# Front of an attention-and-experts kernel: part buffers, the place of unit 0's loads, later constant rows, where the casts run, and when row-max tiles start

## The reference, cut to what matters

```python
q = (x @ Wq).reshape(B, T, N_HEAD, HEAD_DIM).transpose(0, 2, 1, 3)
k = (x @ Wk).reshape(B, T, N_HEAD_KV, HEAD_DIM).transpose(0, 2, 1, 3)
v = (x @ Wv).reshape(B, T, N_HEAD_KV, HEAD_DIM).transpose(0, 2, 1, 3)
...
att = jnp.einsum('bhqd,bhkd->bhqk', q, k) * scale
att = att + alibi[None] + causal[None, None]
att = jax.nn.softmax(att.astype(jnp.float32), axis=-1)
y = jnp.einsum('bhqk,bhkd->bhqd', att, v)
...
x = _layernorm(x + attention(x))
x = _layernorm(x + ffn(x))      # top-1 router, 8 experts, shared expert
```

## Time and profile before

| | us |
|---|---|
| median of 3 runs | 575.14 |
| lowest, highest | 573.35, 577.24 |
| the profiled execution | 570.18 |
| its span, first to last instruction | 568.5 |

### The profile page before, as it was taken

One profiled execution on the slowest core, in us unless ns is written; L12 is line 12 of the kernel. 1 busy time (PEld: TensorE's weight loads), 2 busy tenths in 40 slices (PEclk: granted clock), 3 DMA queues, 4 the chain that ended last, 5 costly groups with the idle time before them and its releaser, 6 DMA issues.

```text
span 568.5 us, 7844 instructions
## 1 busy us (share of the span) xinstructions
PE 520.3 (92%) x2538; PEld 258.0 (45%) x2538; DVE 301.4 (53%) x630; ACT 223.3 (39%) x455; POOL 172.5 (30%) x240
## 2 busy tenths in 40 slices
PE   5858899999999999998987989999989999999991
PEld 2323233333333333332235664655666666656561
DVE  1449988888888888884025635212222332333332
ACT  2311067676767676767940012011112222222310
POOL 4421121412121212121201004970003455454543
PEclk9879599999999999999988799999999999999997
DMA  8489330665354536400223800221111212122210
GB/s 242 136 197 267 121 72 21 134 192 137 123 123 136 138 123 126 133 20 21 67 82 102 277 1 1 71 105 48 55 55 57 74 57 82 58 75 65 64 49 28
DMA packets 39374, 55.91 MB, mean 98 GB/s; under 512 B 5801, under 2 KB 26925, under 8 KB 39230
## 3 DMA queue, kind: packets, MB, share of 16 engines
q1 hardware_dynamic: 29706, 31.94, 21.3%
q0 software_dynamic: 5952, 19.56, 11.0%
q10 hardware_dynamic: 3680, 3.94, 2.5%
HBM read 36.72 MB, written 18.51 MB: 97 GB/s over the span
## 4 chain that ended last, share of the span: by engine, by line
PE 80%; DVE 9%; DMA 4%; ACT 3%; issue 1%; SPq 1%; POOL 1%; POOLq 0%; ACTq 0%; DVEq 0%
PE ps L684 14%; PE ps L513 12%; PE ps L488 11%; PE ps L604 10%; PE ps L502 10%; PE ps L703 7%; DVE mx L834 6%; PE ps L615 5%; PE ps L576 3%; PE ps L490 2%; PE ps L695 2%; ACT probs L759 2%; PE ps L593 1%; DMA qk_or_dn<-qparts 1%; DMA qparts<-tmp 1%
## 5 line engine op out<-in xcount | busy, mean ns | idle before, releaser
L834 DVE TENSOR_REDUCE mx<-ps 128x1 f32<-128x512 f32 (+4 forms) x312 | 183.6, 643 | 30.8 <-PE ps L490 22.7
L759 ACT ACTIVATE probs<-ps 128x512 f32<-128x512 f32 x288 | 152.9, 604 | 79.9 <-PE ps L502 79.7
L488 PE MATMUL ps<-qk_or_dn 127*128 127x512 bf16 (+3 forms) x384 | 122.4, 343 | 10.8 <-DMA qk_or_dn<-qparts 6.0
L502 PE MATMUL ps<-qk_or_dn 127*128 127x512 bf16 x288 | 100.5, 380 | 2.7 <-ACT probs L759 2.3
L1083 POOL TENSOR_SCALAR_AFFINE_SELECT probs<-probs 128x512 f32<-128x512 f32 x64 | 40.7, 636 | 175.8 <-ACT probs L759 175.8
L684 PE MATMUL ps<-wgu,tmp 128*128 x184 | 82.9, 593 | 0.1
L488 PEld LDWEIGHTS ps<-qk_or_dn 127*128 127x128 bf16 x384 | 38.0, 100 | 88.3 <-DVE mx L834 70.1
L513 PE MATMUL ps<-probs,Vs 128*32 128x512 f32 x576 | 76.7, 605 | 0.7 <-ACT probs L759 0.7
L490 PE MATMUL ps<-cb 128*128 128x128 bf16 x256 | 53.3, 232 | 0.0
L1015 DVE TENSOR_TENSOR tmp<-tmp,ps 128x512 f32<-128x512 f32 x23 | 15.8, 687 | 64.8 <-PE ps L684 64.8
L1127 POOL DMA_INDIRECT rows<-acc,tok x23 | 22.5, 980 | 87.1 <-DMA out<-rows,tok 44.0
(11 more groups left out here) (111 smaller groups left out, 460.1 us busy)
## 6 DMA issues: line engine op xcount, KB each, us to landing
wgu<-in_gu POOLq DMA_DIRECT2D x8, 1024.0 KB, 6.2
qk_or_dn<-qparts SPq DMA_DIRECT2D x48, 128.0 KB
yT<-yU SPq DMA_DIRECT2D x16, 256.0 KB, 2.1
qk_or_dn<-in_dn SPq DMA_DIRECT2D x8, 512.0 KB, 8.1
qparts<-tmp SPq DMA_DIRECT2D x8, 384.0 KB, 5.1
tmp<-xs SPq DMA_DIRECT2D x23, 128.5 KB, 2.5
tmp<-yT SPq DMA_DIRECT2D x34, 64.0 KB
xs<-rows POOLq DMA_DIRECT2D x1, 2056.0 KB, 12.7
```

Source lines behind the costliest of these rows:

```text
L488: mm = pe.matmul(o, q, K6[k][0:KROWS, k0:k0 + w], start=True, stop=not masked)
L502: pe.matmul(o, K6[k][0:KROWS, kb * P:(kb + 1) * P], Q6[k][0:KROWS, :, qi * P:(qi + 1) * P], start=True, stop=True).then_inc(s_st, 1)
L759: act.activation(probs[:, 4 * (s % 3) + p, :], ps[:, 4 + (4 * s + p) % SB, :], ACT.Exp, scale=SCALE).then_inc(s_exp, 1)
L834: dve.tensor_reduce(o, ps[:, a_bank(u, t), 0:nh * w].rearrange("p (h w) -> p h w", h=nh), AX.X, ALU.max).then_inc(s_amax, 1)
```

## The change

`parts0` becomes four buffers (`NP`), and `rest0` two. Unit 0's head and its constant rows are issued first, with nothing to wait for; its K and Q loads directly behind the store of job 3, once the four stores have landed, then unit 1's constant rows and head; unit 1's K and Q stay behind the stores of jobs 8 and 9 (`UNIT1_AT`), with unit 2's constant rows behind those. `FIRST_A` is 6: the tiles come in six lots. `LATE_AT` keeps the six later loads at jobs 9, 10, 11. From job 6 on (`ACT_CASTS`) the cast is done by ScalarE at the end of its job step. `s_one` is one semaphore per set, waited for by each unit's first tile.

```diff
--- before.py
+++ after.py
@@ -91,7 +91,10 @@
     (2, 1), (3, 1)]
 NJ = len(JOBS)
 UNIT0_JOBS = 4
-FIRST_A = 8
+NP = 4
+assert UNIT0_JOBS == NP and NJ % NP == 0
+FIRST_A = 6
+UNIT1_AT, LATE_AT, ACT_CASTS = 8, 9, 6
 A_TILES = row_max_tiles()
 NA = len(A_TILES) + 1
 GROUPS = 9
@@ -168,10 +171,10 @@
         cb = sb("cb", [P, CB_N], BF16)
 
         tmp = sb("tmp", [P, 4096 + 2 * (C + 1)])
-        t16 = tmp[:, 0:3 * 3 * CH // 2].bitcast(BF16)
-        parts0 = [t16[:, r * 3 * CH:(r + 1) * 3 * CH].rearrange("p (a t) -> p a t", a=3) for r in range(3)]
-        vT = tmp[NG * D:P, 3840:3840 + CH]
-        rest0 = [tmp[:, 2304 + r * CH:2304 + (r + 1) * CH] for r in range(3)]
+        t16 = tmp[:, 0:NP * 3 * CH // 2].bitcast(BF16)
+        parts0 = [t16[:, r * 3 * CH:(r + 1) * 3 * CH].rearrange("p (a t) -> p a t", a=3) for r in range(NP)]
+        rest0 = [tmp[:, 3072 + r * CH:3072 + (r + 1) * CH] for r in range(2)]
+        vT = tmp[NG * D:P, 4096:4096 + CH]
         yTc = [tmp[:, i * 1024:(i + 1) * 1024].rearrange("p (k t) -> p k t", k=KC) for i in range(3)]
         rdc = [tmp[0:NH, 3072 + i * CH:3072 + (i + 1) * CH] for i in range(2)]
         den = tmp[:, 4096:4096 + 256]
@@ -234,8 +237,8 @@
         s_xT = [sem(f"s_xT{i}") for i in range(NCH)]
         s_prj, s_ph, s_pr, s_pm, s_pl, s_vT, s_vps, s_vev = (
             sem(n) for n in ("s_prj", "s_ph", "s_pr", "s_pm", "s_pl", "s_vT", "s_vps", "s_vev"))
-        s_pw = [sem(f"s_pw{i}") for i in range(3)]
-        s_one, s_seen = sem("s_one"), sem("s_seen")
+        s_pw = [sem(f"s_pw{i}") for i in range(NP)]
+        s_one, s_seen = [sem(f"s_one{i}") for i in range(STEP)], sem("s_seen")
         s_qk = [sem(f"s_qk{i}") for i in range(STEP)]
         s_vinit, s_vs = sem("s_vinit"), sem("s_vs")
         s_aps, s_amax, s_split, s_mparts, s_mrow = (
@@ -347,6 +350,13 @@
                     max_rows(u + 1, (k + 1) % STEP, isinstance(u, int) and u == NU - 2)
                 store_y(u, 1)
 
+            def load_rows(i):
+
+                sp.dma_start(Q6[i][M_ROWS:ROW0, :, :].rearrange("p h t -> p (h t)"), one_d).then_inc(s_one[i], 16)
+                sp.dma_start(K6[i][0:M_ROWS, :], one_d[0:M_ROWS, 0:T]).then_inc(s_one[i], 16)
+                sp.dma_start(Q6[i][TH0:KROWS, :, :].rearrange("p h t -> p (h t)"), thq_d).then_inc(s_one[i], 16)
+                sp.dma_start(K6[i][TH0:KROWS, :], thk_d).then_inc(s_one[i], 16)
+
             def load_x(c):
                 sp.dma_start(xTc[:, c], xT_d[:, c * CH:(c + 1) * CH].rearrange("(k p) t -> p k t", p=P)
                              ).then_inc(s_xT[c], 16)
@@ -360,11 +370,8 @@
             sp.dma_start(cb[:], cb_d).then_inc(s_w0, 16)
             load_x(2)
             load_x(3)
-            for i in range(STEP):
-                sp.dma_start(Q6[i][M_ROWS:ROW0, :, :].rearrange("p h t -> p (h t)"), one_d).then_inc(s_one, 16)
-                sp.dma_start(K6[i][0:M_ROWS, :], one_d[0:M_ROWS, 0:T]).then_inc(s_one, 16)
-                sp.dma_start(Q6[i][TH0:KROWS, :, :].rearrange("p h t -> p (h t)"), thq_d).then_inc(s_one, 16)
-                sp.dma_start(K6[i][TH0:KROWS, :], thk_d).then_inc(s_one, 16)
+            load_rows(0)
+            load_unit_head(0, 0)
             for n in range(NJ):
                 sp.wait_ge(s_pl, n + 1)
                 c, k = JOBS[n]
@@ -374,21 +381,21 @@
                 else:
                     r, m, dst = b * NG * D, NG * D, kparts_d
                 sp.dma_start(dst[:, r:r + m, col:col + CH].rearrange("a r t -> r a t"),
-                             parts0[n % 3][0:m, :, :]).then_inc(s_pw[n % 3], 16)
-                if n == UNIT0_JOBS:
-                    for i in range(3):
-                        sp.wait_ge(s_pw[i], 16 * ((UNIT0_JOBS + 2 - i) // 3))
-                    load_unit_head(0, 0)
+                             parts0[n % NP][0:m, :, :]).then_inc(s_pw[n % NP], 16)
+                if n == UNIT0_JOBS - 1:
+                    for i in range(NP):
+                        sp.wait_ge(s_pw[i], 16)
                     load_unit_k(0, 0)
-                if n == UNIT0_JOBS + 1:
                     load_unit_q(0, 0)
-                if n == FIRST_A:
+                    load_rows(1)
                     load_unit_head(1, 1)
+                if n == UNIT1_AT:
                     load_unit_k(1, 1)
-                if n == FIRST_A + 1:
+                if n == UNIT1_AT + 1:
                     load_unit_q(1, 1)
-            for i in range(3):
-                sp.wait_ge(s_pw[i], 16 * NJ // 3)
+                    load_rows(2)
+            for i in range(NP):
+                sp.wait_ge(s_pw[i], 16 * NJ // NP)
             max_rows(0, 0)
             with sp.Fori(0, LOOPS, 1) as it:
                 for k in range(STEP):
@@ -517,6 +524,8 @@
             def some(todo, n):
                 for v, t in todo[:n]:
                     if t == 0:
+                        if v < STEP:
+                            pe.wait_ge(s_one[v], 64)
                         pe.wait_ge(s_qk[v % STEP], S_QK * (v // STEP + 1))
                     max_tile(v, v % STEP, t)
                 del todo[:n]
@@ -544,7 +553,7 @@
                 if n and JOBS[n - 1][1] == 2:
                     values(JOBS[n - 1][0])
                 if n == FIRST_A + 1:
-                    pe.wait_ge(s_one, 64 * STEP)
+                    pe.wait_ge(s_one[0], 64)
                     pe.wait_ge(s_qk[0], S_QK)
                 if n > FIRST_A:
                     for t in first_tiles(n - 1):
@@ -734,14 +743,20 @@
 
             later_loads = [(x_all[:], x_d, s_x), (wo[:], wo_d, s_wo), (rt[:], rt_d, s_wo), (wsg[:], sg_d, s_wsh),
                            (wsu[:], su_d, s_wsh), (wsd[:], sd_d, s_wsh)]
+            def cast_rest(n):
+
+                m = P if JOBS[n][1] < 2 else NG * D
+                act.wait_ge(s_pr, n + 1)
+                act.activation(parts0[n % NP][0:m, 1, :], rest0[n % 2][0:m, :], ACT.Copy).then_inc(s_pm, 1)
+
             for n in range(NJ):
                 c, k = JOBS[n]
                 m = P if k < 2 else NG * D
                 act.wait_ge(s_prj, n + 1)
-                if n >= 3:
-                    act.wait_ge(s_pw[n % 3], 16 * (n // 3))
-                act.activation(parts0[n % 3][0:m, 0, :], ps[0:m, 4 + n % 4, :], ACT.Copy).then_inc(s_ph, 1)
-                i = 2 * (n - FIRST_A - 1)
+                if n >= NP:
+                    act.wait_ge(s_pw[n % NP], 16 * (n // NP))
+                act.activation(parts0[n % NP][0:m, 0, :], ps[0:m, 4 + n % 4, :], ACT.Copy).then_inc(s_ph, 1)
+                i = 2 * (n - LATE_AT)
                 for dst, src, done in later_loads[i:i + 2] if i >= 0 else []:
                     act.dma_start(dst, src.rearrange("(k p) n -> p k n", p=P)).then_inc(done, 16)
                 if k == 2:
@@ -750,6 +765,8 @@
                     act.activation(vT, ps[NG * D:P, 4 + n % 4, :], ACT.Copy).then_inc(s_vT, 1)
                 if n and JOBS[n - 1][1] == 2:
                     put_values(JOBS[n - 1][0])
+                if n >= ACT_CASTS:
+                    cast_rest(n)
 
             def weights(u, s):
                 for p in range(4):
@@ -836,13 +853,14 @@
 
             for n in range(NJ):
                 m = P if JOBS[n][1] < 2 else NG * D
-                h, md, rest = parts0[n % 3][0:m, 0, :], parts0[n % 3][0:m, 1, :], rest0[n % 3][0:m, :]
+                h, md, rest = parts0[n % NP][0:m, 0, :], parts0[n % NP][0:m, 1, :], rest0[n % 2][0:m, :]
                 dve.wait_ge(s_ph, n + 1)
-                if n >= 3:
-                    dve.wait_ge(s_pl, n - 2)
+                if n >= 2:
+                    dve.wait_ge(s_pl, n - 1)
                 dve.tensor_tensor(rest, ps[0:m, 4 + n % 4, :], h, ALU.subtract).then_inc(s_pr, 1)
-                dve.wait_ge(s_pr, n + 1)
-                dve.tensor_copy(md, rest).then_inc(s_pm, 1)
+                if n < ACT_CASTS:
+                    dve.wait_ge(s_pr, n + 1)
+                    dve.tensor_copy(md, rest).then_inc(s_pm, 1)
                 if n >= FIRST_A:
                     for t in first_tiles(n):
                         reduce_tile(0, t)
@@ -1051,7 +1069,7 @@
             for n in range(NJ):
                 m = P if JOBS[n][1] < 2 else NG * D
                 pool.wait_ge(s_pm, n + 1)
-                pool.tensor_tensor(parts0[n % 3][0:m, 2, :], rest0[n % 3][0:m, :], parts0[n % 3][0:m, 1, :],
+                pool.tensor_tensor(parts0[n % NP][0:m, 2, :], rest0[n % 2][0:m, :], parts0[n % NP][0:m, 1, :],
                                    ALU.subtract).then_inc(s_pl, 1)
             pool.wait_ge(s_vinit, 2)
             pool.wait_ge(s_vev, NCH)
```

## The result

| | before | after |
|---|---|---|
| median, beside each other on one chip | 574.80 us (573.35 to 577.24) | 584.93 us (583.91 to 585.27) |
| profiled execution; its span | 570.18; 568.5 | 585.27; 583.5 |
| first score matmul starts | 71.3 | 75.4 |
| first to last score matmul | 218.2 | 223.5 |
| last score matmul to the end | 279.0 | 284.6 |

The ratio is 1.0169 [1.0131, 1.0207]. The forecast was 571.7 and at most 575.8. All three parts of the span grew: the front by 4.1 us, the middle, which I had called unchanged, by 5.3, and the end by 5.6.

The account below looks back on a forecast made before the run. Front bound by a buffer wait and transfers until 37.7, then VectorE; VectorE would end at 29.8 + 1.1 + 25.2 + 3.75 = 59.85, but the last store sets scores at 67.9, 3.4 us earlier: median 571.7, range 566.0 to 575.8.

Parts of the forecast that it names:

- Four buffers: Front, job 3: its copy no longer waits for a store, so its store is issued at 19.2, not 21.99.
- Unit 0's loads behind its stores: Front, SP's queue: unit 0's Q lands at 29.8 against 37.7, 7.9 us gained.
- spent between 77 and 78, 7.3 us after the first issue: Unit 2's load, the same nine transfers alone, taken as measure for unit 0's landing: 21.9 + 7.3 = 29.2.
- rival 2: Front: gain eaten in transfers, unit 0's Q at 33.6 or later landings 3 us late; gain -0.5 to 1, 575; chance 0.09.
- The price inside VectorE's stretch: Front, VectorE: 25.2 us of work plus 3.75 us of idling, 1.85 of it at job 8.
- the other place: Front, chunk 3's transposes behind job 10 wait for ScalarE's vT of job 9: cost 1.9 us, 0 if wo's issue is short.
- What is late next: End of front: unit 1's Q costs 0.5 us, the last store delays the maxima; scores start at 67.9, not 71.3.
- 11 us after its first issue: Unit 1's Q: landing time read from the trace of before, near 57.5; now near 60, wanted at about 59.5.
- by 66.6 with the worst landing seen (8.9 us): Job 11's store, issued at 57.7, ahead of the maxima: latest landing 66.6, 64.8 taken.
- The middle unchanged: Long middle: TensorE busy 58.49 of 60 us at full clock, so it can't make up or lose time.
- Rival 3 (the clock): Front: TensorE's clock at half for most of the stage makes it the bound; 1.5 to 2.5 us slower, 577; chance 0.07.
- Rivals 1 and 4: Front: 1, gain nearly whole, 568, chance 0.25; 4, job 3's copy held by something else, 574.6, chance 0.02.

Follow-up runs that it names:

- e3: The changed kernel with SP waiting for unit 0's operands before issuing unit 1's constant rows and the stores of jobs 4 to 6: 581.05 us, 1.0157 to before.
- e4: The changed kernel with the six later loads issued by GpSimd in units 0 and 1, not by ScalarE: 575.26 us, 1.0023 to before.
- g2: The changed kernel with only the six later loads moved, issued by GpSimd from unit 6 on: 572.82 us, 0.9958 to before.
- h1: The changed kernel with 16 satisfied waits (eight instructions) ahead of ScalarE's loop and FIRST_A 7, later loads left in place: 573.64 us, 1.0004 to before.
- e1: The kernel before with ten satisfied waits (five instructions) added ahead of ScalarE's loop: 581.22 us, 1.0118 to before.
- e2: The changed kernel with 16 satisfied waits (eight instructions) added ahead of ScalarE's loop: 577.91 us, 1.0067 to before.

## Why the prediction was wrong

The sum for the medians: front +4.1 to +4.5 (71.3 and 70.9 in two profiles of before, 75.4 after; 3 to 3.5 of it by the change, counted from job 1's store), loop +5.3, which leaves 0.3 to 0.7 of the measured 10.1 for the end. Front and loop are single profiles here, so the split is good to about 1 us.

**Four buffers: right.** The copy of job 3 waits for no store, and the store goes out at 20.05 (19.2 forecast; 18.57 to 20.27 over the runs with the new order).

**Unit 0's loads behind its stores: mechanism right, the term mis-sized.** The step that failed is "spent between 77 and 78, 7.3 us after the first issue". I took the fall of the throughput for the landing. There the last load was issued at about 75.7 (three K loads stood behind Q), and the trace of before itself had the tail that e3 shows: SP's queue still moves packets until 80, as in (columns as in the earlier trace rows)

```profile
78.00:79.00 1.00, 1.00 (x11) 0.31 (x4) 0.70 (x2) 0.34 (x1) 0.06 (x1) 1.00 0.23 74
```

and only at 80 are all DMA engines idle, nearly 10 us after the first issue. In e3 a few engines carry the last packets for 2 us after the throughput has fallen. From the last Q issue to its landing it was 6.86 us, nearly the upper bound's 6.63, not 2.8: Q at 34.2, not 29.8, a gain of 3.4 and not 7.9. Job 5's store, ahead of Q before and behind it now, made no difference that shows: 6.63 to 6.85 us in the five profiles with the old order of loads, 6.66 to 8.29 in the nine with the new one. The sign that the prediction had named for rival 2, Q landing after 32, came true.

**The price inside VectorE's stretch: right in sum.** 28.1 us from first to last reduction against 28.95 worked out; job 8's idle 2.20 (1.85 forecast), the other place 0.53 (1.9 forecast; wo's issue held ScalarE 2.06 us, not 3, and e4, without that issue, has the same 0.53). VectorE ended at 63.5; with Q's error of 4.4 us put in, my own sum gives 64.3.

**What is late next: the right place, too small.** Forecast for the first score was 67.9. The 4.4 us by which unit 0's Q was late move nearly everything behind it (x at 45.95 for 42.3, unit 1's Q at 52.75 for 48.9), which gives 72.3 at most; the remaining 3.1 us are the landings. The step that failed is "11 us after its first issue": unit 1's Q took 14.6. And "by 66.6 with the worst landing seen (8.9 us)": the last store took 10.9 and the one before it 13.7. A landing time seen in another mixture of transfers is no upper bound. e4 and g2 show that the later loads are what it collides with (4.4 and 4.9 us), h1 that one lot of tiles fewer in front gives as much back at the first score and 3.5 us at the last. Rival 2 names this; it had 0.09, and it stopped at 3 us of lateness and at a time about that of before (575).

**"The middle unchanged": wrong, and no rival named it.** The argument was that TensorE is full there. What failed is that step: TensorE also depends on ScalarE, whose code had moved. 5.3 of the 10.1 us are this, and by e1 up to 6.6. With the gap taken out (e2) the change is still slower, by 0.67% [0.23, 1.11], where 0.6% faster was forecast; so both failures count.

**Rival 3 (the clock)** held in part: the clock was 0.50 from 60 to 68, but TensorE had 2.91 us of work in those 8 and waited for transfers, so it was not what set the end. **Rivals 1 and 4** did not hold.

## What to carry to other kernels

When straight code ahead of a hardware loop changes by even five instructions, look at the first jump back in the trace of every engine: a gap named "issue" there, with more instruction packets beside it than in a version without the gap, points to a fetch of code. Here five harmless instructions ahead of the loop made it (e1) and eight took it away (e2). Read a landing from the wait that it releases, counted from the last issue, and not from the fall of the throughput. Before work is moved in front of an engine's in-order copies, list every DMA issued behind them, and take loads that are wanted 250 us later out of the stretch in which the critical ones fly.

## What the runs showed that I had not expected

- A jump back to the same loop of 263 instructions costs ScalarE 4.4 to 4.6 us or nothing, by how many instructions stand ahead (60 against 49, 54, 55 and 68); five more of them cost the kernel before 1.2% of its time (e1).
- Nine loads of 960 KB in all keep every DMA engine busy at 133 to 195 GB/s and then leave a tail of 2 us at a sixth of them or fewer; the last is complete 6.7 us after its issue with nothing else in flight.
- The three 384 KB stores issued from 47 us on took 2.5, 6.1 and 3.8 us in e4 and 7.8, 13.7 and 10.9 us in after, by what else was in flight.
- VectorE's stall in the shared expert comes and goes between profiles of the same kernel, whose end was 4.6 us longer in the one with it; the profile shown of before was one of the two without it.
